# Splitting the routed experts' blocks into first and second choices in an RWKV + mixture-of-experts layer

## The reference, cut to what matters

```python
x = x + layernorm(rwkv(layernorm(x)))            # x: (8, 2048, 256) float32, N = 16384 tokens
x = x + layernorm(moe(layernorm(x)))

def moe(xf):                                     # xf: (n, 256), 8 experts, 2 choices per token
    probs = softmax(xf @ router_w)
    topw, topi = top_k(probs, 2)
    combine = zeros((n, 8)).at[arange(n)[:, None], topi].add(topw)
    h = silu(einsum('nd,edf->nef', xf, w1))
    routed = einsum('ne,ned->nd', combine, einsum('nef,efd->ned', h, w2))
    gate, up = split(xf @ shared_gate_up)
    shared = sigmoid(xf @ shared_gate_w) * ((silu(gate) * up) @ shared_down)
    return routed + shared
```

## Time and profile before

| | |
|---|---|
| time, median of 3 runs | 1823.32 us (1821.41 to 1824.04) |
| profiled execution | 1822.15 us, its span 1820.0 us, mean granted clock 0.927 |
| PE, DVE, ACT, POOL busy | 1514.6, 1469.1, 1393.5, 1074.7 us |
| bytes moved by DMA | 274.67 MB |
| first load of the block loop | 1128.8 us |
| last accumulating scatter ends issuing | 1654.0 us |

### The profile page before, as it was taken

The page is one execution under the profiler, slowest core; times in us unless marked ns, Lnnn a source line. Parts: engine busy times, 40 slices in busy tenths (PEclk is TensorE's granted clock), DMA queues, the critical chain, the costliest instruction groups (busy, mean ns, idle before and its releaser), DMA issues.

```text
span 1820.0 us, 34848 instructions
## 1 busy us (share of the span) xinstructions
PE 1514.6 (83%) x9764; PEld 1345.2 (74%) x9764; DVE 1469.1 (81%) x3533; ACT 1393.5 (77%) x2577; POOL 1074.7 (59%) x985
## 2 busy tenths in 40 slices
PE   4899999999999999999999835999999999980000
PEld 3678888888888888888888734999888888870000
DVE  4799989999998989989898754887776777764888
ACT  3799999999999999999999863776666666651444
POOL 1245545455564645556464441688888888886556
PEclk8999999999999999999999966999999999995555
DMA  5123434343332433333342234898888888877997
GB/s 202 47 89 115 139 116 133 118 148 102 118 128 97 142 106 128 109 116 122 106 142 84 93 108 151 243 189 148 145 145 145 144 144 145 147 114 230 415 417 305
DMA packets 184044, 274.67 MB, mean 151 GB/s; under 512 B 17713, under 2 KB 139569, under 8 KB 183857
## 3 DMA queue, kind: packets, MB, share of 16 engines
q1 hardware_dynamic: 132688, 201.37, 32.6%
q0 software_dynamic: 51168, 71.07, 22.1%
HBM read 127.53 MB, written 144.85 MB: 150 GB/s over the span
## 4 chain that ended last, share of the span: by engine, by line
PE 54%; issue 11%; POOL 11%; DMA 8%; DVE 7%; ACT 3%; DVEq 1%; SPq 1%; ACTq 0%; POOLq 0%
PE PS L1289 42%; POOL d_y L547 8%; PE PS L1281 3%; PE PS L1465 3%; PE PS L1483 2%; POOL d_xd L522 2%; DMA d_y<-x,ixb 2%; PE PS L1352 1%; DMA al<-d_y 1%; DMA shh<-d_y 1%; DMA d_y<-nx,ixb 1%; PE PS L1350 1%; DVE bst L881 1%; PE PS L1443 1%; DVEq L1244 1%
## 5 line engine op out<-in xcount | busy, mean ns | idle before, releaser
L522 POOL DMA_INDIRECT d_xd<-h2n,ixs x256 | 321.2, 1255 | 275.1 <-DVE h2n L1060 194.4
L1289 PE MATMUL PS<-hTh,wqh 128*128 128x512 f32 x768 | 306.5, 399 | 15.8 <-ACT kk L581 10.5
L1289 PE MATMUL PS<-hTh,wql 128*128 128x512 f32 x768 | 306.6, 399 | 0.0
L1289 PE MATMUL PS<-hTl,wqh 128*128 128x512 f32 x768 | 306.2, 399 | 0.0
L1289 PEld LDWEIGHTS PS<-hTh,wqh 128*128 128x128 f32 x768 | 146.4, 191 | 50.7 <-ACT kk L581 11.4
L547 POOL DMA_INDIRECT d_y<-xin,ixb x90 | 141.7, 1575 | 52.6 <-DVE xin L1235 27.0
L1289 PEld LDWEIGHTS PS<-hTh,wql 128*128 128x128 f32 x768 | 146.2, 190 | 34.6
L1289 PEld LDWEIGHTS PS<-hTl,wqh 128*128 128x128 f32 x768 | 146.1, 190 | 33.6
L547 POOL DMA_INDIRECT d_y<-x,ixb x90 | 142.3, 1581 | 27.4 <-issue 20.7
L547 POOL DMA_INDIRECT d_y<-nx,ixb x90 | 141.5, 1572 | 27.4 <-issue 22.6
L482 POOL TENSOR_SCALAR var<-mv 128x4 f32<-128x4 f32 x64 | 62.5, 977 | 148.9 <-DVE mv L886 148.7
(11 more groups left out here) (301 smaller groups left out, 5630.5 us busy)
## 6 DMA issues: line engine op xcount, KB each, us to landing
d_y<-ysh SPq DMA_DIRECT2D x64, 512.0 KB
xin<-in_L_attn_x SPq DMA_DIRECT2D x32, 512.0 KB, 3.9
x<-in_L_attn_x SPq DMA_DIRECT2D x32, 512.0 KB, 3.9
d_x<-x SPq DMA_DIRECT2D x32, 512.0 KB
kk<-d_xd SPq DMA_DIRECT2D x34, 272.0 KB
vv<-d_xd SPq DMA_DIRECT2D x34, 272.0 KB
tr<-d_xd SPq DMA_DIRECT2D x34, 272.0 KB
dl<-d_xd SPq DMA_DIRECT2D x33, 272.0 KB
```

The lines of the kernel that those rows point to most:

```text
L522: g.indirect_dma_start(d_xd, bass.IndirectOffsetOnAxis(ap=ixs[:, k:k + 1], axis=0), h2n[:, j, :], None).then_inc(s_sct, 16)
L1289: ins = mm_(out_ap, l, r, start=(k == 0), stop=(k == len(todo) - 1))
```

## The change

- **Blocks by choice.** `d_xd` becomes two tensors, one for first and one for second choices. Positions, counts and block tables get an axis of two. The block loop runs over 71 blocks of first choices (`NB1` = 64 + 7), then 71 of second choices: `NB` = 142.
- **One row of results per token.** `d_y` has N rows. The shared output `ysh`, at full weight, goes to a third tensor `d_xs` in the order of the first choices: POOL scatters it with four more indirect DMAs per chunk (`shared_scatter`), and SP's two stores of it are gone. In blocks of first choices SP loads the shared rows into the result buffer (`load_shared`), DVE multiplies and adds in one instruction, and POOL scatters without accumulation. Before the first block of second choices POOL waits until all of these have landed; then it accumulates as before. Stage C loads one tensor instead of two, `total` is gone, and 14 residual chunks are loaded in the block loop instead of 12.
- **Zero blocks.** SP writes three fixed ones and 8 of the first choices before the block loop, and 8 of the second choices inside it (`tail_2`); ACT issues 8 for `d_xs` after its last `shared_out`. That one now waits until the scatters of the `ysh` before it have landed.
- **The experts' weights** are split one expert every second iteration, from iteration 17 on ACT and 18 on DVE.
- **Order and banks.** `own_exp` moves behind `alpha`; `weighed` behind `shared`; the second up product ahead of the projection; three PSUM banks are swapped; POOL's loop is rotated by one iteration, which leaves the order as it was, with `shared_scatter` behind `scale_in`.

```diff
-    d_y = nc.dram_tensor("d_y", [2 * N + 1 + NSINK * BLK, D], F32).ap()
+    d_y = nc.dram_tensor("d_y", [N + 1 + NSINK * BLK, D], F32).ap()
...
+    NF = N // BLK
+    NB1 = NF + E - 1
+    NB = 2 * NB1
...
-        pU = [PS[4], PS[3]]
+        pU = [PS[0], PS[3]]
-        pV = [PS[1], PS[5]]
+        pV = [PS[1], PS[0]]
-        pRT, pRK = PS[0], PS[0]
+        pRT, pRK = PS[0], PS[4]
...
-                if on(i - 6):
-                    sp.wait_ge(s_ys, n(i - 6, NT, NT))
-                    for s in range(2):
-                        sp.dma_start(ys_a[s, i - 6], ysh[:, :, :]).then_inc(s_st2, 16)
...
+            def load_shared(b):
+                if b >= NYB:
+                    sp.wait_ge(s_yo[b % NYB], 32 * (b // NYB))
+                r = sp.value_load(tabx[0:1, 0, b:b + 1], min_val=0, max_val=E * CAP)
+                sp.dma_start(yb[b % NYB], d_xs[bass.ds(r, BLK), :].rearrange("(p j) d -> p j d", p=P)
+                             ).then_inc(s_yl[b % NYB], 16)
...
             for b in range(NB):
+                if b == NB1:
+                    sp.wait_ge(s_tail2, 16 * E)
                 load_block(b)
+                if 1 <= b <= E:
+                    tail_2(b - 1)
+                if 0 <= b - 2 < NB1:
+                    load_shared(b - 2)
...
-                    sp.dma_start(y0C[c % NY], y_v[0, c]).then_inc(s_cy2[c % NY], 16)
-                    sp.dma_start(y1C[c % NY], y_v[1, c]).then_inc(s_cy2[c % NY], 16)
+                    sp.dma_start(yC[c % NY], y_v[c]).then_inc(s_yl[c % NY], 16)
...
+            def shared_scatter(m):
+                pool.wait_ge(s_pl, n(m, NPL, L_IX))
+                for j in range(NT):
+                    pool.wait_ge(s_ys, n(m, NT, j + 1))
+                    g.indirect_dma_start(d_xs, bass.IndirectOffsetOnAxis(ap=ixs[:, m % 2, j:j + 1], axis=0),
+                                         ysh[:, j, :], None).then_inc(s_scy, 16)
...
                 if m:
-                    act.wait_ge(s_st2, 32 * m)
+                    act.wait_ge(s_scy, 16 * NT * m)
...
-                if i == NCH + 2:
-                    experts_high(EORDER[0:4])
+                if 17 <= i < 17 + 2 * E and i % 2:
+                    experts_high([(i - 17) // 2])
...
+            act.wait_ge(s_zt, 2)
+            act.wait_ge(s_tab, 1)
+            for e in range(E):
+                r = act.value_load(tail[0:1, 0, e:e + 1], min_val=0, max_val=E * CAP - BLK)
+                A.dma_start(d_xs[bass.ds(r, BLK), :].rearrange("(p j) d -> p j d", p=P), zt[:, :, 0:D]).then_inc(s_tail, 16)
...
+                if m >= 2:
+                    dve.wait_ge(s_sct, 16 * 2 * NT * (m - 1))
+                    dve.wait_ge(s_scy, 16 * NT * (m - 1))
+                V.tensor_copy(ixs[:, m % 2, :], posa[:, :]).then_inc(s_pl, 1)
...
-            def total(c):
-                dve.wait_ge(s_cy2[c % NY], 32 * (c // NY + 1))
-                if c >= NO:
-                    dve.wait_ge(s_out[c % NO], 16 * (c // NO))
-                V.tensor_tensor(oC[c % NO], y0C[c % NY], y1C[c % NY], ALU.add).then_inc(s_sum, 1)
-                dve.wait_ge(s_sum, c + 1)
```

More of the change, by code:

```diff
@@ L52, in rwkv_moe @@
     out_c = out.rearrange("b (c p j) d -> (b c) p (j d)", j=NT, p=P)
[L53 to L58 removed]
+    d_xd = [nc.dram_tensor(f"d_xd{s}", [E * CAP + BLK, XW], F32).ap() for s in range(2)]
+    d_xs = nc.dram_tensor("d_xs", [E * CAP + BLK, D], F32).ap()
+    NSINK = E + NB1 - NF + 1
+    d_y = nc.dram_tensor("d_y", [N + 1 + NSINK * BLK, D], F32).ap()
     with ExitStack() as ctx:
@@ L275, in rwkv_moe @@
         s_yo = [sem(f"s_yo{i}") for i in range(6)]
+        s_yl = [sem(f"s_yl{i}") for i in range(6)]
         s_Tx = sem("s_Tx")
@@ L286, in rwkv_moe @@
         s_y = sem("s_y")
-        s_cx = [sem(f"s_cx{i}") for i in range(12)]
-        s_cy2 = [sem(f"s_cy2{i}") for i in range(6)]
-        s_sum = sem("s_sum")
+        s_cx = [sem(f"s_cx{i}") for i in range(14)]
         s_nrm = sem("s_nrm")
@@ L297, in rwkv_moe @@
         NRO = 7
-        L_POS, L_TB, L_PM, L_POSA, L_IX, L_MT, L_DST = range(1, 8)
-        NPL = 7
+        L_POS, L_TB, L_PM, L_POSA, L_IX, L_DST = range(1, 7)
+        NPL = 6
         W_SUM, W_CWT, W_SG, W_CW = range(2, 6)
@@ L314, in rwkv_moe @@
         hidB, outB = PS[2:5], PS[5:8]
-        zt = xb[1]
+        zt = ee[:, :, :].rearrange("p a t -> p (a t)")[:, 0:2 * XW].rearrange("p (j d) -> p j d", j=2)
         yb = [t[:, i:i + 2, :] for i in (0, 2) for t in (xin, nx, x1)]
         NYB = len(yb)
+        NYL = [(NB1 - i + NYB - 1) // NYB for i in range(NYB)]
+        assert NYB == 6
         xTh = [hTh[:, 0, 0:TC], rkh[:, 0, :]]
@@ L386, in _ @@
             sp.dma_start(x1[:, :, :], x_v[0]).then_inc(s_xr, 16)
-            for i in range(NCH + 6):
+            for i in range(NCH + 4):
                 if i % 2 == 0 and i // 2 < E:
@@ L475, in _ @@
             for e in range(E):
-                last = g.memset(tb[:, e:e + 1], float(e * CAP))
+                last = g.memset(tb[:, :, e:e + 1], float(e * CAP))
             last.then_inc(s_const, 1)
@@ L521, in scatter @@
                     k = s * NT + j
[L522 removed]
+                    g.indirect_dma_start(d_xd[s], bass.IndirectOffsetOnAxis(ap=ixs[:, m % 2, k:k + 1], axis=0),
                                          h2n[:, j, :], None).then_inc(s_sct, 16)
[L525 to L526 removed]
+            def shared_scatter(m):
[4 more added lines that the diff above has]
+                                         ysh[:, j, :], None).then_inc(s_scy, 16)
+            scale_in(0)
+            for i in range(NCH + 6):
+                if i == NCH + 3:
+                    pool.wait_ge(s_rkh, NCH)
+                    pool.wait_ge(s_rkl, NCH)
+                    g.memset(zt[:, :, 0:D + E], 0.0).then_inc(s_zt, 1)
+                    g.tensor_copy(zt[:, :, D + E:XW], sinki[:, :, :]).then_inc(s_zt, 1)
+                if on(i - 4):
+                    scale_o(i - 4)
+                if on(i - 5):
+                    scatter(i - 5, 0)
+                    scatter(i - 5, 1)
+                if on(i - 4):
+                    scale_h2(i - 4)
                 if 0 < i < NCH:
                     scale_in(i)
[L529 to L541 removed]
+                if on(i - 6):
+                    shared_scatter(i - 6)
             for w in range(NB):
@@ L1158, in _ @@
                 if on(i - 3):
+                    weighed(i - 3)
                     sums(i - 3)
@@ L1193, in _ @@
             step(4)
-            V.tensor_tensor_scan(cum[:, :], ones8[:, :], nbk[:, :], zero[:, 0:1], ALU.mult, ALU.add).then_inc(s_tb, 1)
-            V.tensor_scalar(wstep[:, :], nbk[:, :], -float(BLK), float(CAP), ALU.mult, ALU.add).then_inc(s_tb, 1)
-            step(6)
-            V.tensor_tensor(big[:, :, :], iotb[:, :].unsqueeze(2).to_broadcast([P, NBP, E]),
-                            cum[:, :].unsqueeze(1).to_broadcast([P, NBP, E]), ALU.is_ge).then_inc(s_tb, 1)
+            for s in range(2):
+                V.tensor_tensor_scan(cum[:, s, :], ones8[:, :], nbk[:, s, :], zero[:, 0:1], ALU.mult, ALU.add).then_inc(s_tb, 1)
```

256 lines of the change are left out of this document (131 added, 125 removed).

## The result

The changed kernel takes 1845.8 us (median of 4 runs, 1841.1 to 1846.4) against 1823.2 us before: a ratio of 1.0117, with a 95% interval of 1.0105 to 1.013. The forecast was 1797 us and faster, with a range to 1818. The profiled execution has a span of 1844.7 us.

The account below looks back on a forecast made before the run. It took PE to bound stage A, POOL's accumulating scatters the block loop, and DMA bytes most of stage C. Terms +2 (stage A), +7 (drain), +6 (blocks), -40 (stage C) gave -25: span 1795, time 1797 us, range 1777 to 1818.

Parts of the forecast that it names:

- First half of the blocks: Block loop, 71 blocks with plain scatters: PE sets the pace at 3.38 us per block, 240 us.
- the 3 us for the residuals: Block loop: residual loads added in 14 blocks cost 0.25 us each, +3 us, with bounds of nothing to +7.
- 3 us between the halves: Block loop: POOL waits some 3 us between the halves for the last plain scatter to land.
- The rival of a slower first half: First half stays near POOL's or DMA's rate, 3.6 to 3.76 us per block, 1813 to 1824 us; chance 0.13.
- Stage A: +2 us: Stage A: PE keeps the pace; the moved split costs 0.25 us in each of 8 chunks, +2 us.
- the bound of +12: Stage A: upper bound of the +2 us term; the lower bound was nothing.
- Between stage A and the loop: +7 us: Drain: splitting gone, -6.5 us, but a chain of shared scatters and zero blocks moves the first load to some 1136; +7 us.
- Second half: 267 us: Block loop, 71 blocks of second choices: POOL's pace, 142 accumulating scatters at 1.88 us each, 267 us.
- Stage C: -40 us: Stage C: fewer bytes, 73 us to the last residual request, then 14 chunks at 3.5 us; 125.5 us, gain 40.5.
- The rival of no gain in stage C: Stage C gains nothing since y is not what its DMAs wait for; 1837 us; chance 0.03.
- that of stage A's lost rhythm: Stage A: longer POOL loop or place delays h2n past its slack in every chunk; 1831 us at 1.2 each; chance 0.11.
- 1.1 us of slack: Stage A: h2n ends at 926.73 and PE wants it at 927.8, so 1.1 us per chunk may be lost.

Follow-up runs that it names:

- e3_acc: Changed kernel with accumulating scatters in the first 71 blocks too, and x1 tiles also stored into y in stage A: 1825.8 us, first half 278.8 us.
- e7_direct: Changed kernel with ordinary stores in place of the plain indirect scatters, rows of y not in token order: 1796.3 us, first half 246.6 us.
- e18_shift: Changed kernel with both scatters of each first-half block waiting until DVE has read weights four blocks on: 1803.6 us, first half 252.9 us.
- e10_behind: Changed kernel with two 420-element POOL clears behind the second scatter of each first-half block: 1845.4 us, first half 293.0 us.
- e17_drain: Changed kernel with only the split of the experts' weights put back to the end of stage A: 1791.1 us, first half 250.0 us.
- e8_zero: Changed kernel with ACT's eight zero blocks issued ahead of its last shared_out: 1840.2 us, first half 297.5 us.
- e5_noself: Changed kernel without PE's three waits for its own work in the block loop: 1826.8 us, ratio to before 1.0023, first half 272.7 us.

## Why the prediction was wrong, step by step

**First half of the blocks: the step that failed.** "So these blocks go at PE's rate: 71 x 3.38 = 240 us." Measured 296.2; with the 3 us for the residuals and 3 us between the halves 246 were forecast, so this one term is off by 50 us of the 49.7 that the span misses. The step took an engine with the most busy time, and no other over it, to be the pace, and it had no term for PE's waits for its own and others' waits for its signals. The failed assumption is that PE's end and its signal are the same. Shown is: signals of PE come late in the slow rhythm, the product's by 0.68 us and the transposes' by 0.18 us on average, together about the time lost per block; plain indirect scatters of POOL are needed for it (with accumulation, e3_acc, or ordinary stores, e7_direct, no signal is late and the loop runs at POOL's or at PE's pace); moving the pair against PE's block takes it away (e18_shift), adding the same work without moving it does not (e10_behind); the shared loads add 0.27 us per block within it. The rate that I forecast, 246 us with its additions, is nearly there in the fast rhythm: 249 to 253 us.

**The rival of a slower first half** was named, at 3.6 to 3.76 us per block and 1813 to 1824 us. It had the right stretch and the right direction, but its mechanism (full DMA engines) was wrong: the DMA share is 0.69 at 4.16 us per block and 0.78 at 3.41. Both its rate and its time were exceeded.

**Stage A: +2 us, measured more.** PE reaches `ranks` of chunk 28 at 1010.4 us, before at 1001.1: +9.3. The eight chunks with a split take 32.3 to 34.4 us, those between them 31.7 to 31.8. With the split put back they are 31.8 again, which shows the cause. It lies within the bound of +12 that I gave; 0.25 us for each was too little.

**Between stage A and the loop: +7 us, measured +0.4.** From that point on the drain was 12.4 us shorter (6.5 forecast), and from the last `ranks` to the first block load 12.8 us longer (13.5 forecast). The load came at 1138.49 us, forecast 1128.8 + 2 + 7 = 1137.8. That the two terms together came out right is luck: stage A cost 7.3 us more than forecast, and the stretch behind it 6.6 us less. The chain behind the last scatters is the one I wrote down (timelines of ACT, its queue and SP's):

```profile
1124.76 1.57 ACT L645 ACTIVATE ysh<-PS,ssum 128x256 f32<-128x256 f32 x4 [14.92 <-DMA d_xs<-ysh,ixs]
1125.85 9.95 ACTq L854 DMA_DIRECT2D d_xs<-ee  x8
...
1138.49 0.37 SPq L429 DMA_DIRECT2D kk<-d_xd  x1
```

ACT waits 14.92 us for the shared scatters to land and then needs 9.95 us for its zero blocks. Drain and stage A together did not pay: with the split put back (e17_drain) the last `ranks` comes 6.7 us earlier, at 1096.6 us against 1103.3.

**Second half: 267 us, measured 267.7. Stage C: -40 us, measured 124.8 us against 166.0, -41.2.** The second half went as written: POOL again at 1.55 us and 0.30 us per accumulating scatter. In stage C two misses cancel. The last residual is asked for 77.2 us into the stage (73 forecast; 261 GB/s in 1722 to 1740 us, 414 in 1740 to 1800), and the rest took 47.6 us (52.5 forecast), since the last chunks follow each other at 2.9 us where nothing is missing, DVE's own time and not the 3.5 I took. The rival of no gain in stage C is out, and so is that of stage A's lost rhythm: 1.1 us of slack held in the chunks without a split.

**Open.** Why PE's signals come late beside plain scatters is not shown. That the product ends inside a second scatter goes with it in every slow trace but is not enough by itself (e17_drain and e18_shift above). Nor is it shown why e17_drain falls into the fast rhythm and e8_zero, whose first scatter comes at nearly the same time (1149.3 and 1149.7 us), into the slow one; e17_drain was run once, the changed kernel four times with the same result. That moving the pair is what helps rests on e18_shift, one run, with e10_behind against it.

## What to carry to other kernels

- When no engine is full in a loop, ask which signal is late: compare the start of the last instruction before it with the instant at which two different waiters go on. PE waiting for its own product was the sign here.
- A loop in which POOL's scatters follow PE's product and PE waits for it again can settle into a slow rhythm. Shift or space the scatters (a later wait, a clear behind each) and time it, before pricing engines; an edit far from the loop can flip it too, by 46 us here (one run).
- A split that lengthens eight chunks of the stage that is full costs more than the same split in a drain with idle engines, even on its chain: 6.7 us here.

## What the runs showed of the hardware that was not expected

- PE's completion signals were seen up to 3 us after the start of the last matmul (e5_noself), with PE running on. In the changed kernel 47 of 51 products' signals were over 0.1 us late; with stores in place of the scatters (e7_direct) none of 190 signals of PE was. ACT's and DVE's signals in the same rows were on time: in the second scatter of 1177.59 to 1178.55, ACT's copy ends at 1177.87 and its semaphore changes at 1177.88.
- A plain scatter of 128 rows takes POOL 0.96 us and an accumulating one 1.55 us; the former was still the slower choice in the changed kernel, 4.16 against 3.77 us per block (e3_acc).
- 840 elements cleared per block on POOL, 0.9 us of added work, took 44 us off the first half.
